# A message-passing layer on one core: packed plan words, a short path on TensorE, and attribute splits three groups ahead

## The reference

```python
x0 = relu(layernorm(x))                       # 1250 nodes x 512
edge_emb = edge_attr @ W_edge + b_edge        # 20000 edges, 128 -> 512
msg  = relu(x0[src] + edge_emb)
aggr = segment_sum(msg, dst, 1250)            # dst sorted; dst = int(1250 * u**2)
h = (1 + eps) * x0 + aggr
h = gelu(layer_norm(h @ W1 + b1, g1, be1))    # 512 -> 1024
h = gelu(layer_norm(h @ W2 + b2, g2, be2))    # 1024 -> 512
h = layer_norm(x0 + h, gA, bA)
m = gelu(h @ M1) @ M2
out = x + layer_norm(h + m, gB, bB)
```

## Time and profile before

| | us |
|---|---|
| median of 3 runs | 567.51 |
| lowest, highest | 563.29, 567.92 |
| the profiled execution, as timed | 562.67 |
| its span in the profile | 560.8 |
| PE busy | 471.7 (84%) |
| DVE busy | 407.6 (73%) |
| ACT busy | 300.4 (54%) |
| POOL busy | 325.4 (58%) |
| mean granted clock of TensorE | 0.957 of full speed |

### The profile page before, as it was taken

The page is one execution under the profiler, slowest core; times in us unless marked ns, Lnnn a source line. Parts: engine busy times, 40 slices in busy tenths (PEclk is TensorE's granted clock), DMA queues, the critical chain, the costliest instruction groups (busy, mean ns, idle before and its releaser), DMA issues.

```text
span 560.8 us, 7864 instructions
## 1 busy us (share of the span) xinstructions
PE 471.7 (84%) x1915; PEld 348.7 (62%) x1916; DVE 407.6 (73%) x550; ACT 300.4 (54%) x569; POOL 325.4 (58%) x306
## 2 busy tenths in 40 slices
PE   1072999989679898898867999999998699999994
PEld 0041666656346565465546887778877589888883
DVE  7852999887379696688892888879999844472465
ACT  3742787786186786878881544455554555014000
POOL 4675788887588778888830444427777542240152
PEclk9997899989789899899989999999999799999998
DMA  8677567677667766669404522244442031121022
GB/s 279 240 210 225 181 200 233 206 220 212 192 198 209 212 203 205 193 201 348 125 1 176 207 79 79 116 151 128 148 136 76 0 97 55 39 85 29 21 92 75
DMA packets 31416, 85.26 MB, mean 152 GB/s; under 512 B 4592, under 2 KB 4928, under 8 KB 31360
## 3 DMA queue, kind: packets, MB, share of 16 engines
q0 software_dynamic: 12560, 41.17, 24.9%
q1 hardware_dynamic: 17984, 42.74, 22.2%
q10 hardware_dynamic: 816, 0.77, 0.5%
HBM read 72.07 MB, written 5.24 MB: 138 GB/s over the span
## 4 chain that ended last, share of the span: by engine, by line
PE 39%; DVE 24%; issue 19%; ACT 8%; POOL 4%; ACTq 3%; DMA 2%; DVEq 1%; another core or an unknown queue 1%; POOLq 0%
PE ps_t L1155 5%; DVE msg_lo L953 5%; DVE work L1022 5%; PE ps_u L1131 5%; PE ps_u L1129 5%; PE ps_u L1130 5%; PE ps_u L1139 4%; DVE z L948 4%; PE ps_t L1130 4%; PE ps_t L1131 4%; PE ps_t L1129 4%; POOL rstd L534 3%; ACTq L297 2%; ACT squares L755 2%; PE ps_t L1139 2%
## 5 line engine op out<-in xcount | busy, mean ns | idle before, releaser
L521 POOL DMA_INDIRECT rows<-gather_table,src_idx x157 | 190.6, 1214 | 60.4 <-issue 42.4
L697 ACT ACTIVATE msg_hi<-z 128x1024 fp32r<-128x1024 f32 (+1 forms) x79 | 82.8, 1048 | 67.7 <-DVE z L948 42.4
L953 DVE SCALAR_TENSOR_TENSOR msg_lo<-z,msg_hi 128x1024 fp32r<-128x1024 f32 (+1 forms) x79 | 100.8, 1277 | 0.7 <-ACT msg_hi L697 0.7
L1139 PE MATMUL ps_u<-we_raw,attr_raw 128*128 128x512 f32 x104 | 58.7, 648 | 39.7 <-issue 24.4
L532 POOL TENSOR_TENSOR var_eps<-mv,eps_t 128x1 f32<-128x1 f32 x40 | 11.5, 289 | 133.4 <-DVE mv L1010 68.4
L948 DVE TENSOR_TENSOR z<-ps_u,rows 128x1024 f32<-128x1024 f32 (+1 forms) x53 | 64.1, 1209 | 32.0 <-issue 14.7
L1129 PE MATMUL ps_u<-w_hi,lhs_lo 128*128 128x512 f32 x160 | 64.7, 405 | 4.2 <-DVE lhs_lo L1001 3.0
L1131 PE MATMUL ps_u<-w_hi,lhs_hi 128*128 128x512 f32 x160 | 62.9, 393 | 0.0
L1130 PE MATMUL ps_u<-w_lo,lhs_hi 128*128 128x512 f32 x160 | 62.8, 392 | 0.0
L1155 PE MATMUL ps_t<-msg_lo,onehot 128*128 128x512 f32 x145 | 60.7, 419 | 0.0
L1155 PE MATMUL ps_t<-msg_hi,onehot 128*128 128x512 f32 x145 | 57.7, 398 | 0.0
(11 more groups left out here) (158 smaller groups left out, 1056.9 us busy)
## 6 DMA issues: line engine op xcount, KB each, us to landing
attr_raw<-in_attr_t SPq DMA_DIRECT2D x20, 512.0 KB
w_raw<-in_W SPq DMA_DIRECT2D x24, 256.0 KB, 2.7
tile_in<-mid SPq DMA_DIRECT2D x10, 512.0 KB, 3.3
res<-in_x SPq DMA_DIRECT2D x20, 256.0 KB, 2.7
xin<-in_x SPq DMA_DIRECT2D x5, 512.0 KB, 7.4
gather_table<-tab SPq DMA_DIRECT2D x5, 512.0 KB, 2.8
out<-work SPq DMA_DIRECT2D x10, 256.0 KB, 2.1
rows<-gather_table,src_idx POOLq DMA_INDIRECT x157
```

What stands on the lines that cost most here:

```text
L521: g.indirect_dma_start(rows[:, group.r, e % TPG, :], None, gather_table[:, :], bass.IndirectOffsetOnAxis(src_idx[:, e:e + 1].bitcast(u32), ...
L697: a.activation(pair(msg_hi, g, p), summed(g, p), ACT.Relu).then_inc(msg_hi_done, 1)
L953: v.scalar_tensor_tensor(pair(msg_lo, g, p), summed(g, p), 0.0, pair(msg_hi, g, p).bitcast(f32), ALU.max, ALU.subtract).then_inc(msg_lo_do ...
L1139: t.matmul(o[:, D:2 * D], attr_raw[:, g.k, (2 * p + 1) * P:(2 * p + 2) * P], we_raw[:, :], start=True, stop=True)
```

## The change

- The plan is packed: eight words for each group, most of them several bit fields. EVENT holds 0 for a group without an event, else one number with the first window, the last window, a flag for a changed window and three bits each for the tiles that touch the last and the first window. The word beside it is the bank. COUNTS holds the three running numbers that PE waits for, SCALAR all that ACT needs for its flags, the window to close and its numbers, LATE and the word behind it what ACT needs when it closes in the middle. Fields are cut out with shifts and masks, and a window's bank follows from its number, so `w_bank` is gone.
- PE reads 2 words for each group, and one more at an event. The scatter of pair 0 is written out twice: with a test for each tile if the group has an event, without tests if not. The scatter of pair 1 always visits both tiles.
- ACT reads 1 word for each group, and at an event no other, but two words where it closes in the middle.
- `attr_hi` is a ring of three instead of two, and ACT makes it three groups ahead. `attr_lo` stays a ring of two.
- DVE makes the first `attr_lo` before it computes the plan.
- The bias column of `apart` is addressed by the group's number alone, with the tile as a constant.

```diff
-(EVENT, BANK, TOUCH_LAST, _, _, LO, BEFORE, COUNT, CHANGED, BANK_LO, BANK_NEXT, RUN, EXTRA, THIRD, CROSSING, ...
- PLAN) = range(27)
+EVENT, COUNTS, SCALAR, LATE, PLAN = 0, 2, 3, 4, 8
...
-        attr_hi = sb("attr_hi", [P, 2, SPLIT], f32r, edge)
+        attr_hi = sb("attr_hi", [P, RING, SPLIT], f32r, edge)
...
+        def field(word, first, bits):
+            return (word >> first) & ((1 << bits) - 1)
+
+        def bank_of(w):
+            return nc.s_assert_within((w & 1) * D, 0, D, ...)
...
             def split_attr(g):
                 act.wait_ge(attr_in[g.k // 2], 16 * (g.attr_lap + 1))
-                if not zero(g.gr, 1):
-                    act.wait_ge(emb_done[1], g.gr - 1)
-                a.activation(by_pair(attr_hi[:, g.q, :]), ...
+                if not zero(g.gr, RING - 1):
+                    act.wait_ge(emb_done[1], g.gr - RING + 1)
+                a.activation(by_pair(attr_hi[:, g.r, :]), ...
...
-                    last = a.activation(apart[:, e, :], iota[:, 0:P], ACT.Square, bias=neg_rel_last[:, ds(g.gr * TPG + e, 1)])
+                    last = a.activation(apart[:, e, :], iota[:, 0:P], ACT.Square, bias=neg_rel_last[:, ds(g.gr, 1), e:e + 1]...)
...
-            def events(gr, q, loaded=None):
-                with nullcontext() if loaded else act.If(plan_part(ENG.Activation, gr, ANY, 1, 2 * NT)[0] > 0):
-                    late, final, cross, w, number, bank = loaded or flags_of(gr)
+            def events(gr, q, word=None):
+                with nullcontext() if word is not None else act.If((loaded := word_of(gr)) & 7 > 0):
+                    word = loaded if word is None else word
...
-                        with act.If(late > 0):
-                            lo, before, count, changed = plan_part(ENG.Activation, gr - 1, LO, 4, NT)
-                            _, extra, third, _ = plan_part(ENG.Activation, gr - 1, RUN, 4, NG * NT + 1, least=1)
+                        with act.If(word & 2 > 0):
+                            spans, counts = plan_words(ENG.Activation, gr - 1, LATE, 2)
...
-                            select_first(gr, q, plan_part(ENG.Activation, gr, CROSSING, 1, NG + 1, least=1)[0])
+                            select_first(gr, q, field(word, 16, 6))
...
-                if not (isinstance(g.gr, int) and g.gr >= NG - 2):
-                    split_attr(g.next(2))
+                if not (isinstance(g.gr, int) and g.gr >= NG - RING):
+                    split_attr(g.next(RING))
                 events(g.gr, g.q)
...
+            split_attr(fixed(0))          # DVE, now ahead of the plan
...
-            def scatter_extra(g, event):
+            def scatter_extra(g, word):
                 tiles = list(range(g.tiles - 1, -1, -1))
-                with pe.If(event > 0):
-                    lo, _, count, changed, bank_lo_now, bank_next = plan_part(ENG.PE, g.gr, LO, 6, max(NT, D))
-                    run, _, third, crossing, *touched = plan_part(ENG.PE, g.gr, RUN, 3 + TPG, NG * NT + 1)
+                with pe.If(word > 0):
+                    counts = plan_words(ENG.PE, g.gr, COUNTS)[0]
+                    lo, run = held(field(word, 0, 4), NT - 1), held(field(counts, 0, 9), NG * NT + 1)
+                    count = field(word, 4, 4) - lo + 1
                     pe.wait_ge(msg_lo_done, 2 * g.gr + g.pairs)
...
-            def scatter_last(g, p, bank, touched):
+            def scatter_last(g, p, word, bank):
                 if p == 0:
                     pe.wait_ge(onehot_ready, g.gr + 1)
                 pe.wait_ge(msg_lo_done, 2 * g.gr + p + 1)
-                last = visit(onehot[g.r], g, bank, range(2 * p, 2 * p + g.in_pair(p)), g.tiles - 1, touched)
-                if p == g.pairs - 1:
-                    last.then_inc(scattered, 1)
+                tiles = range(2 * p, 2 * p + g.in_pair(p))
+                if p == 0 and g.pairs == 2:
+                    with pe.If(word > 0):
+                        visit(onehot[g.r], g, bank, tiles, g.tiles - 1, [word & 1 << 9 + e for e in tiles])
+                    with pe.Else():
+                        visit(onehot[g.r], g, bank, tiles, g.tiles - 1)
+                else:
+                    visit(onehot[g.r], g, bank, tiles, g.tiles - 1).then_inc(scattered, 1)
...
-                    event, bank, *touched = plan_part(ENG.PE, before.gr, EVENT, 1 + TPG, D)
+                    word, bank = plan_words(ENG.PE, before.gr, EVENT, 2)
```

More of the change, by code:

```diff
@@ L294, in pair, with plan_words @@
             return t[:, g.r, 2 * D * p:D * (2 * p + g.in_pair(p))]
[L296 to L308, removed]
+        def plan_words(engine, gr, c, n=1):
+            _, words = nc.values_load_multi_w_load_instructions(
+                plan[0:1, ds(gr, 1), c:c + n].rearrange("p a c -> p (a c)"), engines=[engine], min_val=0, max_val=(1 << 24) - 1,
+                skip_runtime_bounds_check_because="the plan is built of fields of fixed widths")
+            return words
+        def field(word, first, bits):
+            return (word >> first) & ((1 << bits) - 1)
+        def bank_of(w):
+            return nc.s_assert_within((w & 1) * D, 0, D, skip_runtime_bounds_check_because="the plan has the two halves")
         def window(w):
             return nc.s_assert_within(w, 0, NT - 1, skip_runtime_bounds_check_because="the plan is clamped to the windows")
-        def half(bank):
-            return nc.s_assert_within(bank, 0, D, skip_runtime_bounds_check_because="the plan has the two halves")
         def zero(i, k=0):
@@ L602, in _ @@
             a.activation(we_hi[:, :], we_raw[:, :], ACT.Copy).then_inc(we_hi_ready, 1)
[L603 to L604 removed]
+            for gr in range(RING):
+                split_attr(fixed(gr))
             def w1_high(c):
@@ L679, in events @@
                                 act.wait_ge(scattered, gr - 1)
                                 alone(act)
-                                close(window(before), bank_of(ENG.Activation, window(before))).then_inc(closed, 1)
+                                close(window(before), bank_of(before)).then_inc(closed, 1)
+                            count = hi - lo + 1
                             with act.If(count > 2):
@@ L1180, in extra_window @@
                         begin(window(lo + k), banks[1])
-                    with pe.If(changed > 0):
+                    with pe.If(word & 1 << 8 > 0):
                         pe.wait_ge(closed, run)
                         alone(pe)
-                        begin(window(lo), half(bank_lo_now))
+                        begin(window(lo), bank_of(lo))
                     with pe.If(count > 1):
-                        pe.wait_ge(first_ready, crossing + 1)
+                        pe.wait_ge(first_ready, field(counts, 9, 6) + 1)
                         alone(pe)
-                        extra_window(1, onehot_first[g.q], (half(bank_lo_now), half(bank_next)), [None] + touched)
+                        extra_window(1, onehot_first[g.q], (bank_of(lo), bank_of(lo + 1)), [None] + [word & 1 << 12 + e for e in range(TPG - 1)])
                         with pe.If(count > 2):
+                            third = field(counts, 15, 9)
                             with pe.Fori(2, count) as k:
@@ L1207, in step @@
                 if before:
-                    event, bank, *touched = plan_part(ENG.PE, before.gr, EVENT, 1 + TPG, D)
+                    word, bank = plan_words(ENG.PE, before.gr, EVENT, 2)
+                    bank = nc.s_assert_within(bank, 0, D, skip_runtime_bounds_check_because="the plan has the two halves")
                 for p in range(2):
```

165 lines of the change are left out of this document (85 added, 80 removed).

## The result

| | before | after |
|---|---|---|
| median of 20 runs each, taken side by side | 565.06 us | 562.89 us |
| lowest to highest | 560.51 to 568.16 | 555.93 to 568.03 |
| ratio, with its 95% interval | | 0.9945 [0.9919, 0.9971] |

The change saves 0.55%, 3.1 us, where 10 us were forecast. The ratio compares the fast executions alone, and the profiled one of after, 565.5 us, is not among them. Where a few us of after's trace matter, the second trace of each kernel stands beside it.

A forecast was written before the change was run, and what follows sets the result against it. PE and DVE were taken to trail POOL's gathers by 8.4 to 11 us; 14 us saved closes this, leaving POOL as bound. The stage ends 10.7 us earlier, rounded to 10: 567.5 - 10 = 557.5 us, range 545 to 568.

The forecast's parts named there:

- Plan loads on PE with a median under 0.7 us: Sign on PE: two event loads of 3.16 us become one of one word, taken as 0.3 us.
- The idle time ahead of an event's first matmul: PE at events: 2.0 us earlier each; of 14.1 us idle, 11 us go and under 4 stay.
- The wait of DVE for attr_hi: DVE in the edge stage: 6.3 us in 4 pieces gone, counting only with PE's idle, which it overlaps.
- The sum of 14 us off PE and DVE: Edge stage after 154 us: about 9.2 us from PE's terms plus some 5 from attr_hi and ACT waits.
- The front, 0: First attr_lo made before the plan: gain of 0 to 2 us possible at the first z, taken as 0.
- The load ahead of neg_shift: ACT at the stage's end: 2.95 us idle for loads, 1.8 seen by PE; gain taken as 0.7 us.
- the 9.5 us behind the last z: End of the edge stage: 9.5 us expected to follow the last z, where 12.4 us stood before.
- Gathers no slower: POOL: gathers get no faster, not averaging over 1.6 us; last rows 2.4 us later, at 278 to 281.
- the rival in which gathers grow beside a denser DVE: POOL takes the gain: gathers grow from 1.56 to 1.62 us, gain only 5, time 562.5 us; chance 0.20.
- So the lag is closed: End of the edge stage: 14 us saved covers the lag of 8.4 to 11 us, so POOL bounds the stage.
- Long waits of PE's signals at other places: Sign that the prediction is wrong: long waits for PE's signals come elsewhere in the trace; no size given.
- a gain from the pieces following one another: Stage end: POOL's four w_lo pieces (4.92 us for two) run successively beside DVE's last msg_lo, helping reach 9.5 us.

The follow-up runs named there:

- half kernels: Kernel before and changed kernel, both without gathers of odd tiles: 539.02 and 522.38 us; repeated on another chip, 537.16 and 521.70 us.
- half_before_two: Kernel before without the gathers of the odd tiles, repeated on a chip with late signals: 537.16 us, ratio 0.9577.
- ring_only: Kernel before with only attr_hi as a ring of three, made three groups ahead: 566.06 us, ratio 0.9999.
- before_same: Kernel before, unchanged, traced on a second chip beside the changed kernel: one execution, 565.02 us.
- after_same: Changed kernel, unaltered, run again on a second chip against the kernel before: 562.55 us, ratio 0.9994.
- look4: Changed kernel with GpSimd gathering four pairs ahead of z, not six: 551.10 us, ratio 0.9924.
- look4_same: Changed kernel with GpSimd four pairs ahead, not six, repeated on a chip with late signals: 557.27 us, ratio 0.9898.
- look3: Changed kernel with GpSimd gathering three pairs ahead of z, not six: 552.56 us, ratio 0.9960.
- half_after: Changed kernel without the gathers of the odd tiles: 522.38 us, ratio 0.9401 against the kernel before.
- half_after_two: Changed kernel without the gathers of the odd tiles, repeated on a chip with late signals: 521.70 us, ratio 0.9302.
- filler: Changed kernel with each gather replaced by a GpSimd add of two constant tiles, no DMA: one execution, 569.88 us.

## Why the prediction was wrong, point by point

Right were the steps that take time off PE, ACT and DVE.

- Plan loads on PE with a median under 0.7 us: 0.54.
- The idle time ahead of an event's first matmul: 2.47 us became 0.63 in the event shown. In the half kernels, which no late signal blurs, the eight pieces of 14.9 us became six of 6.9. That is 8 us off, where the prediction took 11 and under 4 left. In the whole kernel the total stayed 12.3, with one piece of 5.3 us in it.
- The wait of DVE for attr_hi, taken as 6.3 us and gone: gone in after, and worth more where it counts, 15.6 us in 11 pieces in half_before_two. ring_only shows that it is worth nothing by itself in the whole kernel.
- The sum of 14 us off PE and DVE: measured as 16.6 and 15.5 us with half the gathers, of which 2.8 and 2.9 are the earlier first z; from the first z to the last it is 14.1 and 13.6.
- The front, 0: z starts 2.2 us earlier, and the late signals that follow swallow it: the z that ends them starts at 55.8 us in before and at 58.5 in after.
- The load ahead of neg_shift: it waits 1.39 us for 2.95. But the 9.5 us behind the last z did not come. In after neg_shift, at 298.38, no longer marks the end of the stage, as PE still scatters until 301.1 us. PE turns the first node tile 302.24 - 291.21 = 11.0 us behind the last z, for 12.4 in before:

```profile
299.76 1.09 PE L1259 MATMUL ps_t<-ident,acc 128*128 128x128 f32 x8 [1.84 <-ACT neg_shift L724]
```
```profile
302.24 1.09 PE L1278 MATMUL ps_t<-ident,acc 128*128 128x128 f32 x8 [1.13 <-DVE acc L995]
```

- Gathers no slower: 1.24 us a gather for 1.25. The last rows landed at 281.2 us, at the top of the forecast 278 to 281. But by the same reading before's landed at 276.4 (2.2 us behind the last gather, not 4.64), so they came 4.8 us later, where 2.4 were forecast; GpSimd waited for z 17.8 us for 13.8. So the rival in which gathers grow beside a denser DVE has the right time, 562.5 us, by luck: its mechanism did not happen, and it counts from 567.5 us, which 20 runs put at 565.06.

**The step that failed is "So the lag is closed".** The lag is how far z of the last pair starts behind the landing of its rows. It is 10.0 us in after (291.2 - 281.2), where less than 2 were forecast, and was 10.9 in before (287.3 - 276.4). The prediction took it as the sum of PE's and ACT's waits at events, which 14 us more than covers. The end of the stage (PE's first node tile) is the sum of three parts, in us:

| trace | last rows landed | lag of the last z | last z to first node tile | end |
|---|---|---|---|---|
| before | 276.4 | 10.9 | 12.4 | 299.8 |
| after | 281.2 | 10.0 | 11.0 | 302.2 |
| before_same | 275.2 | 13.3 | 12.5 | 301.0 |
| after_same | 275.0 | 11.0 | 12.0 | 298.0 |

The change took 0.9 and 2.3 us off the lag, not 8 or more. The runs put three things in its place.

1. Late signals. In before they already cost DVE 21.2 us, more than the event loads cost PE, and the two long waits of POOL in the earlier trace rows were their ends, not a matter of GpSimd. In after they cost 39.9, 18.7 us more, and on the second chip 31.3 for 25.2, 6.1 more. How much they grow is not settled: over all traces with six pairs they cost 21 to 28 us in the kernel before and its variants, 24 to 41 in the changed kernel and its variants. That they took back the saved time is argued from this and from GpSimd's longer waits for z, not shown apart. "Long waits of PE's signals at other places" was named as what would make the prediction wrong, but stood in none of the cases.
2. The rows. With signals in time (look4) z waits 30.9 us for rows, and from 61 to 230 us every z starts within 2.3 us of their landing: the gathers bound the stage, as forecast, and this is why 16 us off the other engines can't all reach the end. So late signals are not needed for a small gain: look4, the change with the shorter lead, saved 0.76%, 4.2 us, on the chip without them.
3. A part of the lag was never PE's. POOL's first two w_lo pieces start right behind the last gather, and beside them DVE takes 5.60 us for a msg_lo of 1.22 and 2.24 for an attr_lo of 0.45:

```profile
278.99 5.60 DVE L967 SCALAR_TENSOR_TENSOR msg_lo<-z,msg_hi 128x1024 fp32r<-128x1024 f32 x1
284.51 1.21 DVE L962 TENSOR_TENSOR z<-ps_u,rows 128x1024 f32<-128x1024 f32 x1
285.64 2.24 DVE L871 TENSOR_TENSOR attr_lo<-attr_raw,attr_hi 128x256 fp32r<-128x256 f32 x1
```
```profile
278.76 4.73 POOL L525 TENSOR_TENSOR w_lo<-w_raw,w_hi 128x1024 fp32r<-128x1024 f32 x2
285.25 2.35 POOL L525 TENSOR_TENSOR w_lo<-w_raw,w_hi 128x1024 fp32r<-128x1024 f32 x1 [1.76 <-ACT w_hi L607]
```

The msg_lo ends 1.1 us behind both w_lo pieces: it stood until they had ended. That is 4.4 + 1.8 = 6.2 us ahead of the last z. In before it was 3.0 (an attr_lo of 1.24 and a msg_lo of 3.39 us in the same place). So 3.0 of before's lag could not be won this way. It is no matter of late signals: in look4 the last z is 8.3 us behind its rows all the same, with one attr_lo of 5.05 us beside three pieces:

```profile
264.86 1.23 DVE L962 TENSOR_TENSOR z<-ps_u,rows 128x1024 f32<-128x1024 f32 x1 [1.98 <-issue]
266.00 5.05 DVE L871 TENSOR_TENSOR attr_lo<-attr_raw,attr_hi 128x256 fp32r<-128x256 f32 x1
```
```profile
263.73 7.03 POOL L525 TENSOR_TENSOR w_lo<-w_raw,w_hi 128x1024 fp32r<-128x1024 f32 x3
```

Counted in the same way it is 4.3 us in after_same, 5.9 in look4_same and 6.5 in look3. The prediction had the 4.92 us of the earlier trace rows in its hand and expected a gain from the pieces following one another; where three of them do, DVE stands longest (attr_lo of 5.05, 6.28 and 6.89 us in look4, look4_same and look3). That moving w_lo behind the last z gains these 6 us is argued, not tried.

What makes a signal late stays open. Shown is that it goes with gathers: none late with half of them (four traces, two of them on a chip that has late signals), none with adds in their place. It does not go with their bytes, nor with an unbroken row of them. Shown too is that it depends on the chip: none in two kernels with all gathers where before takes 555 us, late ones in each of the 13 others with all gathers, which took 557 to 567 us. That the late signals alone make the 10 us between such chips is likely, but the changed kernel with six pairs was not run on the fast one, and no trace of before was taken there.

One rival stands untested: the recording of the traces. Records of semaphores are missing only in traces from the chips with late signals, and there only beside gathers. Of 2512 records of landing gathers before has 1343 and after 1126, look4 and look3 all; half_after has all of its 1264, half_after_two, on a chip with late signals, 1112. filler, on that chip and without gathers, lacks none of its DMAs' records. From 40 to 60 us, where before and after both have late signals, after has 37 records for 13 gathers, of 208. Either the recording holds the signals up, or what holds them up also loses records; no run here tells these apart.

## What to carry to other kernels

Time saved on an engine reaches the end only if no other wait is refilled from it. So take out half of the work of the suspected bound in both kernels, and compare: here that showed 16 us of worth where the whole kernels showed 0 to 3. Before counting a lag as winnable, split it: what of it is the engine's own idle time, what is an instruction that takes four times its usual duration beside another engine's, and what is a wait whose named releaser had long been done. And when an engine that runs ahead has more lead than it needs, a shorter lead is a one-line test: four pairs for six gave 5.3 us here on one chip, more than the change.

## What the runs showed of the hardware that was not expected

- In all sets but one, signals of finished matmuls came up to 13 us after the modelled end, while GpSimd issued a gather every 1.25 us. With half the gathers or none it did not happen. Records of semaphores were missing in every trace with late signals (1126 of 2512 landings recorded in after, all in look4).
- The same kernel took 555 us on one chip, at a mean granted clock of 0.968, and 563 to 565 on the others, at 0.957 to 0.959.
- DVE's msg_lo, 1.22 us alone, took 5.60 beside two of GpSimd's subtractions of 2.4 us each, and ended 1.1 us behind the second. z, which reads PSUM, kept its 1.23 us beside them (at 264.86 us in look4).
- A register load cost PE 0.31 us for one word and 0.54 for two: 0.23 us a word, as in the earlier trace rows.
